# One block for the routed feed-forward and the agent attention of a two-layer decoder

## The reference, cut to what matters

```python
def _L0_ffn_ref(x, Wg, We, be):               # E = 8, cap = 32 * 112 // 8
    h = x.reshape(n, d)
    probs = jax.nn.softmax(h @ Wg, axis=1)
    mask = jax.nn.one_hot(jnp.argmax(probs, axis=1), E)
    gate = jnp.sum(probs * mask, axis=1)
    locations = jnp.cumsum(mask, axis=0) - 1.0
    mask = mask * (locations < cap)
    # each kept token: gate * (h @ We + be); a token over its expert's capacity: 0
def _L1_attn_ref(x, w_qkv, w_conv1):
    # q, k, v = x @ w_qkv.T in three parts
    agent = jnp.einsum('bnc,c->bn', q, w_conv1)
    agent_attn = softmax(jnp.einsum('bn,bnc->bc', agent * scale, k), axis=-1)
    agent_v = softmax(jnp.einsum('bc,bnc->bn', agent_attn, v), axis=-1)
    agent_v = jnp.einsum('bn,bnc->bc', agent_v, v)
    agent_tok = softmax(agent[:, :, None], axis=-1)
    return agent_tok * agent_v[:, None, :]
```

## Time and profile before

| | us |
|---|---|
| median of 3 runs (3384.04 to 3399.62) | 3393.48 |
| the profiled execution's own time | 3393.12 |
| its span in the trace | 3391.3 |
| first to last instruction of the two blocks and the layernorm between them (1625.58 to 2005.90) | 380.3 |

### The profile page before, as it was taken

How to read it: one execution, slowest core, us unless ns; L and a number is a source line. 1 busy time by engine, 2 the same in 40 slices (tenths; PEclk the granted TensorE clock), 3 DMA queues, 4 the chain that set the end, 5 groups by cost and what they waited for, 6 DMA issues and landing times. The chain is left out here.

```text
span 3391.3 us, 62686 instructions
## 1 busy us (share of the span) xinstructions
PE 2893.5 (85%) x21120; PEld 1909.7 (56%) x21121; DVE 2024.0 (60%) x4546; ACT 1544.2 (46%) x3150; POOL 408.4 (12%) x405
## 2 busy tenths in 40 slices
PE   4788888886699999998886867999999867869994
PEld 1344444443367766776556754777777634436663
DVE  2388888887277777776224344777777634563334
ACT  1465665552266666664112313666666332211222
POOL 0000000000200000000000012011011022214441
PEclk8889999998799999998555578999999889988997
DMA  3000000000000000000000001000000030001115
GB/s 89 0 0 0 0 0 0 0 0 1 26 24 18 18 23 18 18 18 1 4 0 13 0 6 46 19 23 23 18 23 18 1 128 13 12 21 46 64 62 155
DMA packets 57533, 80.49 MB, mean 24 GB/s; under 512 B 8593, under 2 KB 46660, under 8 KB 57092
## 3 DMA queue, kind: packets, MB, share of 16 engines
q1 hardware_dynamic: 51380, 62.55, 6.3%
q0 software_dynamic: 6048, 16.52, 1.5%
HBM read 63.46 MB, written 15.60 MB: 23 GB/s over the span
## 5 line engine op out<-in xcount | busy, mean ns | idle before, releaser
L1016 DVE CUSTOM_DVE_ANT_0 xa_h_scores<-xa_h_score_bank,xa_h_added 112x375 f32<-112x375 f32 x1024 | 518.1, 544 | 152.7 <-PE xa_h_score_bank L951 138.2
L1110 ACT ACTIVATE xa_h_probs<-xa_h_scores,xa_h_negmax 112x375 f32<-112x375 f32 x1024 | 561.4, 600 | 0.8 <-DVE xa_h_negmax L1023 0.6
L963 PEld LDWEIGHTS xa_h_turn_bank<-keep_ident,xa_h_probs 112*125 112x125 f32 x3072 | 398.4, 190 | 91.3 <-ACT xa_h_probs L1110 22.3
L963 PE MATMUL xa_h_turn_bank<-keep_ident,xa_h_probs 112*125 112x112 f32 x3072 | 438.3, 279 | 8.7 <-DVE xa_h_probs_t L1030 8.5
L1030 DVE COPY xa_h_probs_t<-xa_h_turn_bank 125x448 f32<-125x448 f32 x512 | 319.1, 623 | 150.9 <-PE xa_h_turn_bank L963 137.8
L1116 ACT ACTIVATE xa_h_probs_t<-xa_h_turn_bank 125x448 f32<-125x448 f32 x256 | 138.8, 542 | 303.7 <-PE xa_h_turn_bank L963 303.7
L358 PE MATMUL mb_y_bank<-mb_read_out,keep_ident 128*128 128x448 f32 x512 | 231.2, 600 | 25.6 <-DVE mb_read_out L560 25.5
L553 DVE TENSOR_TENSOR_SCAN mb_state<-mb_decay,mb_drive 128x1792 f32<-128x1792 f32 x64 | 248.5, 3883 | 2.1 <-ACT mb_decay L487 2.1
L951 PE MATMUL xa_h_score_bank<-xa_h_keys,xa_h_queries 32*112 32x375 f32 x2048 | 230.9, 520 | 11.4 <-DVE xa_h_row_max L1016 10.7
L976 PEld LDWEIGHTS xa_h_sums_bank<-xa_h_probs_t,xa_h_values 125*32 125x32 f32 x6144 | 141.9, 110 | 154.4 <-DVE xa_h_probs_t L1030 149.2
L976 PE MATMUL xa_h_sums_bank<-xa_h_probs_t,xa_h_values 125*32 125x112 f32 x6144 | 202.6, 265 | 14.6 <-issue 6.3
(11 more groups left out here) (330 smaller groups left out, 4544.4 us busy)
## 6 DMA issues: line engine op xcount, KB each, us to landing
xa_h_context<-in_ctx_t SPq DMA_DIRECT2D x64, 375.0 KB, 3.1
lm_w<-in_m_w SPq DMA_DIRECT2D x16, 512.0 KB
lm_e_wide<-lm_result_rows SPq DMA_DIRECT2D x8, 896.0 KB, 9.5
keep_x<-in_x SPq DMA_DIRECT2D x4, 896.0 KB, 11.2
lm_latent_rows<-lm_rows SPq DMA_DIRECT2D x8, 448.0 KB, 3.2
out_x<-keep_x SPq DMA_DIRECT2D x8, 448.0 KB, 6.1
xa_h_mask_raw<-in_key_mask SPq DMA_DIRECT2D x1, 1312.5 KB
mb_f_pw<-in_pw SPq DMA_DIRECT2D x1, 1024.0 KB
```

What stands on the lines that cost most here:

```text
L963: last = pe.transpose(turn_bank[(par + kc) % 2][0:KP, g * S:(g + 1) * S], probs[par][:, g, kc * KP:(kc + 1) * KP], keep.ident[0:S, 0:S])
L1016: dve.tensor_tensor_reduce(scores[par][:, g, :], score_bank[g][0:S, 0:SK], added[s][:, :], 1.0, -BIG, ALU.add, ALU.max, row_max[par][:, g: ...
L1110: act.activation(probs[par][:, g, :], scores[par][:, g, :], ACT.Exp, bias=negmax[s][:, G * c + g:G * c + g + 1]).then_inc(probs_ready, 1)
```

## The change

The two blocks and the layernorm between them become one block, `switch_and_agent`. It has no loops. Its parts:

- Eight input DMAs stand ahead of the first matmul (four of them the bias, laid out as two rows of 512), and six for the agent's weights behind them.
- Scoring: for all eight groups ScalarE normalises (Identity with a scale and a bias per token), TensorE turns a group into two banks, ScalarE copies them to `normed_t`, which keeps all batches, and TensorE takes the gate logits. All logits stay in one PSUM bank.
- Routing on VectorE: as before, with one scan of 264 elements for the eight of 32.
- The stream, ten steps t: TensorE does the expert matmuls of group t in two halves (one bias matmul of 512 columns for two batches, then four matmuls of 256), turns the new rows of group t-1, sums the channels of group t-2, and takes the agent scores of group t-1. At t = 0 it also works out the agent weight and at t = 1 the places. VectorE updates x straight from PSUM, takes statistics, aggregates them for the group and works out the scale with GpSimd's power of -0.5 and one Newton step. ScalarE normalises the group's new rows into `tokens`, which keeps all batches, and copies the turned rows to `tokens_t`.
- The end, for all batches at once: the channel softmax; 64 matmuls for the token scores from `tokens_t`; the token softmax; 64 matmuls for the gathered sums from `tokens`; one product with the value weight for all batches; and eight groups of four 32-row matmuls that give each batch its row times the token's own factor, added to x by VectorE over 1,024 columns at a time, with the statistics behind.

The diff, cut to its core (removed lines and empty lines are left out; `switch_ffn` and `agent_attention` go):

```diff
+PHASES = (1, 2, 3, 5, 6,)
...
+def switch_and_agent(nc, keep, name, w):
...
+        out_psum = [[banks[0:S, 2 * n + b // 2, b % 2 * D:(b % 2 + 1) * D] for b in range(G)] for n in range(2)]
+        turn_psum = [banks[:, 4 + c, 0:T] for c in range(DC)]
...
+            for r in range(2):
+                for k in range(2):
+                    sp.dma_start(expert_b[32 * r:32 * r + 1, k * D:(k + 1) * D], w["expert_bias"].rearrange("(o n) -> o n", o=1)).then_inc(loaded, 16)
             sp.dma_start(upto[:, :], w["upto"]).then_inc(loaded, 16)
+            sp.dma_start(reset[:, :], w["reset"]).then_inc(loaded, 16)
...
+            sp.dma_start(wq[:, :, :], qkv[0:D, :].rearrange("(c p) n -> p c n", p=128)).then_inc(agent_loaded, 16)
+            sp.dma_start(conv1[:, :], w["conv1"]).then_inc(agent_loaded, 16)
...
+            sp.dma_start(own_batch[:, :], w["own_batch"]).then_inc(agent_loaded, 16)
...
+            def turn_rows(g):
+                pe.wait_ge(normed_ready, G * (g + 1))
+                reuse(pe, turned_read, DC * g)
+                for c in range(DC):
+                    for b in range(G):
+                        last = pe.transpose(turn_psum[c][:, b * S:(b + 1) * S], normed[g % 2][:, b, c * 128:(c + 1) * 128], keep.ident[0:S, 0:S])
+                    last.then_inc(turned, 1)
...
+            def gate_logits(g):
+                pe.wait_ge(turned_read, DC * (g + 1))
+                for b in range(G):
                     for c in range(DC):
+                        last = pe.matmul(logits_psum[:, G * g + b, :], normed_t[:, c, g, b * S:(b + 1) * S], gate_w[:, c, :], start=c == 0, stop=c == DC - 1)
+                last.then_inc(logits_done, 1)
+            def expert(g, half):
+                reuse(pe, updated, G * (g - 2) + 2 * half + 2)
+                bank = banks[0:S, 2 * (g % 2) + half, :]
+                pe.matmul(bank, ones[32 * half:32 * half + 1, :], expert_b[32 * half:32 * half + 1, :], start=True, stop=False)
+                for b in (2 * half, 2 * half + 1):
                     for c in range(DC):
+                        last = pe.matmul(out_psum[g % 2][b], normed_t[:, c, g, b * S:(b + 1) * S], expert_w[:, c, :],
+                                         start=False, stop=b % 2 == 1 and c == DC - 1)
+                last.then_inc(expert_done, 1)
+            def number_places():
+                pe.wait_ge(chosen_ready, 1)
+                pe.matmul(places_psum, upto[:, :], chosen[:, :, 1:], start=True, stop=False)
+                pe.matmul(places_psum, ones[:, :], earlier[:, :, 0:B], start=False, stop=True).then_inc(places_done, 1)
+            def agent_scores(g):
+                pe.wait_ge(tokens_t_ready, DC * (g + 1))
+                reuse(pe, sum_ready, g)
+                for b in range(G):
                     for c in range(DC):
+                        last = pe.matmul(agent_psum[:, b:b + 1], tokens_t[:, c, g, b * S:(b + 1) * S], agent_w[:, c:c + 1], start=c == 0, stop=c == DC - 1)
+                last.then_inc(agent_done, 1)
+            def sum_tokens(g):
+                pe.wait_ge(agent_ready, g + 1)
+                for b in range(G):
                     for c in range(DC):
+                        last = pe.matmul(token_sum_psum[:, c, b:b + 1], tokens[:, G * g + b, c * 128:(c + 1) * 128], agents[:, G * g + b:G * g + b + 1],
                                          start=True, stop=True)
+                last.then_inc(sum_done, 1)
...
+            for g in range(GROUPS):
+                turn_rows(g)
+                if g > 0:
+                    gate_logits(g - 1)
+            gate_logits(GROUPS - 1)
+            for t in range(GROUPS + 2):
+                if in_range(t):
+                    expert(t, 0)
+                    expert(t, 1)
+                if t == 1:
+                    number_places()
+                if in_range(t - 1):
+                    turn_tokens(t - 1)
+                if in_range(t - 2):
+                    sum_tokens(t - 2)
+                if t == 0:
+                    pe.wait_ge(agent_loaded, 16 * 6)
+                    for m in range(DC):
+                        for c in range(DC):
+                            last = pe.matmul(banks[:, 7, m:m + 1], wq[:, c, m * 128:(m + 1) * 128], conv1[:, c:c + 1], start=c == 0, stop=c == DC - 1)
+                    last.then_inc(agent_w_done, 1)
+                    pe.wait_ge(agent_w_ready, 1)
+                if in_range(t - 1):
+                    agent_scores(t - 1)
...
+            pe.wait_ge(own_step, 4)
+            pe.transpose(banks[:, 5, 0:S], own_probs[:, :, :].rearrange("p r b -> p (r b)"), keep.ident[0:S, 0:S]).then_inc(own_step, 1)
+            pe.wait_ge(act_step, 3)
+            for b in range(B):
+                for c in range(DC):
+                    last = pe.matmul(banks[0:S, 3, b:b + 1], tokens_t[:, c, b // G, b % G * S:(b % G + 1) * S], channel_w[:, c, b:b + 1],
                                      start=c == 0, stop=c == DC - 1)
             last.then_inc(pe_step, 1)
+            pe.wait_ge(act_step, 4)
+            pe.transpose(banks[0:B, 0, 0:S], token_scores[:, :], keep.ident[0:S, 0:S]).then_inc(pe_step, 1)
             pe.wait_ge(dve_step, 4)
+            pe.transpose(banks[0:S, 1, 0:B], token_probs[:, :], keep.ident[0:B, 0:B]).then_inc(pe_step, 1)
+            pe.wait_ge(act_step, 6)
+            for b in range(B):
+                for c in range(DC):
+                    last = pe.matmul(banks[:, 2, c * B + b:c * B + b + 1], tokens[:, b, c * 128:(c + 1) * 128], token_weights[:, b:b + 1],
+                                     start=True, stop=True)
+            last.then_inc(pe_step, 1)
+            pe.wait_ge(act_step, 7)
+            for c in range(DC):
+                last = pe.matmul(banks[:, 3, 0:D], gathered[:, c, :, :].rearrange("p r b -> p (r b)"), wv_t[:, c, :], start=c == 0, stop=c == DC - 1)
+            last.then_inc(pe_step, 1)
+            pe.wait_ge(act_step, 8)
+            pe.wait_ge(own_step, 6)
+            for g in range(GROUPS):
+                reuse(pe, x_added, g - 1)
+                for r in range(4):
+                    band = slice(32 * r, 32 * (r + 1))
+                    last = pe.matmul(banks[0:S, 4 * (g % 2) + r, 0:D], own_wide[band, g, :], agent_v[band, :], start=True, stop=True)
+                last.then_inc(value_done, 1)
...
+            def normalise_rows(g):
+                reuse(act, turned, DC * (g - 1))
+                for b in range(G):
+                    t = G * g + b
+                    act.activation(normed[g % 2][:, b, :], keep.x[:, t, :], ACT.Identity, bias=shift[:, t:t + 1],
+                                   scale=keep.rstd[:, t:t + 1]).then_inc(normed_ready, 1)
...
+            for t in range(GROUPS + 2):
+                if in_range(t - 1):
+                    normalise_tokens(t - 1)
+                if in_range(t - 2):
+                    act.wait_ge(sum_done, t - 1)
+                    act.activation(token_sum[:, :, G * (t - 2):G * (t - 1)], token_sum_psum, ACT.Copy).then_inc(sum_ready, 1)
+                if in_range(t - 1):
+                    read_tokens(t - 1)
+                if t == 0:
+                    act.wait_ge(agent_w_done, 1)
+                    act.activation(agent_w[:, :], banks[:, 7, 0:DC], ACT.Copy).then_inc(agent_w_ready, 1)
+                if in_range(t - 1):
+                    act.wait_ge(agent_done, t)
+                    act.activation(agents[:, G * (t - 1):G * t], agent_psum, ACT.Copy, scale=float(D) ** -0.5).then_inc(agent_ready, 1)
...
+            pool.memset(power[:, :], -0.5).then_inc(power_set, 1)
+            pool.wait_ge(power_set, 1)
+            for g in range(GROUPS):
+                here = slice(G * g, G * (g + 1))
+                pool.wait_ge(scaling, SCALING * g + 2)
+                pool.tensor_tensor(rstd2[:, here], variance2[:, here], power[:, :], ALU.pow).then_inc(rooted, 1)
...
+            def update(g, half):
+                dve.wait_ge(expert_done, 2 * g + half + 1)
+                for b in (2 * half, 2 * half + 1):
+                    t = G * g + b
+                    dve.scalar_tensor_tensor(keep.x[:, t, :], out_psum[g % 2][b], weight[:, t:t + 1], keep.x[:, t, :],
                                              ALU.mult, ALU.add).then_inc(updated, 1)
+                for b in (2 * half, 2 * half + 1):
+                    t = G * g + b
                     dve.wait_ge(updated, t + 1)
+                    dve.bn_stats(stats2[:, t, :], keep.x[:, t, :]).then_inc(measured, 1)
+            def scales(g):
+                at, here = SCALING * g, slice(G * g, G * (g + 1))
+                for b in range(G):
+                    dve.wait_ge(measured, G * g + b + 1)
+                    last = dve.bn_aggr(moments2[:, G * g + b, :], stats2[:, G * g + b, :])
+                last.then_inc(scaling, 1)
+                dve.wait_ge(scaling, at + 1)
```

(25 more changed lines are left out.)

512 lines of the change are left out of this document (158 added, 354 removed).

## The result

The changed kernel takes 3295.61 us (median of four, 3287.68 to 3299.82), beside 3389.93 for the kernel before in the same session; the ratio is 0.972, 95% interval 0.969 to 0.975. The forecast was 3283, the range 3234 to 3332. Of the profiled execution of after the span is 3293.8 us, 97.5 less than before. The new block runs from 1622.01 to 1902.57: 280.6 us in place of 380.3, so 99.8 are saved in it, where 110 were forecast. The parts around it are the same code and differ by 3.6 us ahead (less) and 5.8 behind (more).

What follows compares the result with a forecast made beforehand. TensorE's instruction count at half clock was taken as the bound, VectorE's serial part behind it. 306.1 us at 1.2 GHz against 380.3, less 36 for the clock, gave 270, saving 110: 3393.1 to 3283 us, range 3234 to 3332.

Steps and rivals of the forecast that it cites:

- The sum at 1.2 GHz: Whole new block before any rise of the clock: 5.4 + 36.5 + 177.9 + 86.3 = 306.1 us against 380.3.
- Weights: From the block's start until its eight input DMAs have landed: 5.4 us (bounds 5.0 and 6.7).
- scoring: Turns and gate logits of eight groups plus the first copy out of PSUM: 36.5 us, ScalarE hidden.
- end: Behind the stream, from channel softmax to the last update of x: 86.3 us, VectorE bounding its last part.
- The clock gain: In the stream: 23%, taken from the old kernel's third pass, off 154.8 us of TensorE work, 36 us.
- R: Follow-up theory for the stream: one-row bias matmuls keep the clock down; leaving the bias out gives about 3248 us.
- Gap: TensorE idle once ahead of group 0's turns, waiting for the chain that starts at the places: 9.1 us.
- The stream's terms: Stream at 1.2 GHz: eight groups 163, idle 9.1, places 2.3, agent weight 2.1, last handoff 0.7; given as 177.9 us.
- A: Rival: half clock throughout, the stream's dense stretches never raise it; 3319 us, chance 0.20.
- B: Rival: full clock in the stream, half of its 154.8 us of work goes; 3242 us, chance 0.17.
- C: Rival: the stream's groups do not overlap, the chain shows in seven more groups, 46 us; 3329 us, chance 0.06.
- D: Rival: slower, GpSimd's power in software lengthens each group; 25 us a power cancels the saving, 27 gives 3409; chance 0.03.

Runs made afterwards that it cites:

- the serial order: Changed kernel with the overlap of groups undone: turns, scores and sums of group t right behind its experts; 3339.41 us, ratio 0.986 to the kernel before.

## Why the prediction was right, and where it was off

- **The sum at 1.2 GHz held.** Weights, scoring and end came within 0.7, 0.2 and 0.2 us; a group in the stream at 1.2 GHz within 0.1 (20.33 against 20.4), though by luck: the work was 0.4 more than summed and the wait 0.5 less. Prices from the earlier trace rows carried over to new shapes: two records of 512 columns were taken at 1.97, and start to start they are 1.97 (1727.51 to 1729.48).
- **The clock gain was mis-sized, 36 us against 21.7.** The forecast lies 13 us below the time measured, and this term makes 14 of it. The step was to carry the third pass's 23% over to the stream. 23% was within reach of this code: with one small wait moved, PE's busy time from the first expert record on is 110.9 against 131.2 in after and some 153 by the sum at 1.2 GHz, 27% less. But the share is no property of the instructions. The third pass of the earlier trace rows got a rise in each of its eight groups, one every 10.24 us from 1930.11 to 2001.79; in the stream some groups get one and others do not.
- **The reason against it, that one-row biases break the dense stretch, was not the cause.** Three edits of the bias each gained, one by exactly R's number, but each also shortened the groups and so moved them on the grid, and the moved wait and the serial order showed rises in every group with the bias in place. That they came out so near R's numbers was in part luck.
- **Idle time held.** Gap 8.94 against 9.1; waits of 1.14 against 1.6, 8.6 in all against 12.8; one wait was not in the sum, 2.2 us ahead of the last group's turns, where no expert work covers ScalarE's rows. GpSimd's power takes 1.01 us against 0.5, ScalarE's Identity 0.59 against 0.5; the updates and statistics of the gap took 2.9 (1681.29 to 1684.18) against 3.5, which evens it out.
- **Slips in the sums.** The stream's terms (163, 9.1, 2.3, 2.1, 0.7) add up to 177.2 and not 177.9, and the chain's to 9.2 and not 9.1. The sizes that "can add up to 9 us" add up to 16; 8 is what they make when each errs by itself. None of it moves the forecast by a microsecond, but a range built on 16 would have been wider at both ends.
- **The rivals.** A did not hold as a whole, but two of the groups are A. B's full clock appears only when the sums are streamed: with that edit a group takes 10.17 us at 1.00. C, the missing overlap, was priced at 46 and measured at 44 to 49 by undoing it. D would have needed a power of 25 us.

What is shown: the same instructions in the same order cost 13.6 to 20.3 us a group, and a group begun at 1.2 GHz gets its rise or not, and early or late, by where it lies on the grid; a wait of 1 us acts on the clock by moving the groups on it. The Trainium skill, TensorE: Matmul & The Clock Gate, section What's actually happening, says that activity is judged in a rhythm of its own that does not start anew with a kernel; the traces agree, as the changes of the clock keep to one even grid in each of them and this grid lies elsewhere in each. What stays open: a kernel with nothing but one delay ahead of the stream would have moved the place alone; it was not tried. And no run says why the groups with streamed sums stay at 1.00 in two traces and not in two others.

## What to carry to other kernels

Price a change at the lower clock from rows, and treat the clock's gain as a range of its own, as it hangs on where the groups fall in time more than on the count of instructions; one trace is then one draw, so look at several executions. Where many one-column matmuls load data as weights, try swapping the operands: with a stationary tile that is zero but for one column the data streamed at the same price at 1.2 GHz (the sums 3.46 to 3.62 us a group against 3.44) and got the full clock in both blocks of the end. Before covering an idle gap, ask whether the work behind it may then run at the lower clock. When an edit changes the order of matmuls of few rows, see whether they now run side by side, before giving the gain to the clock.

## What was not expected of the hardware

- One-column matmuls keep TensorE in flight for 24.05 and 27.47 us on end at 0.50. The same data streamed in records of 112 or 256 columns takes 14.61 and 15.69.
- Taking 5.5 us of waits from a stream of 151.7 shortened it by 25.7.
- Taking about 9 us of idle time out gave 5.3 in one kernel's stream and nothing that the medians show in another.
- Two bias matmuls of one row each, from rows 0 and 32 and issued one behind the other, take 1.98 us together at 1.2 GHz, and one takes 1.97. At 2.4 GHz it is 1.04 (1674.92 to 1675.96 in that kernel's trace) against 1.03 (1676.06 to 1677.09 in after).
- All rises and falls of the clock in a trace lie on one even grid of times that runs on through idle time.
- A bias of 512 columns over 112 rows is no dearer than one over a single row: 1.82 us from start to start (1724.42 to 1726.24 in that kernel's trace) against 1.97.
- GpSimd's power of 112 x 4 elements takes 1.01 us, about as long as its add of 128 x 448.
